# A graph network's third layer opens its dense hop with four rounds at once on the node chunks that are ready

## The chip, the cores and the metric

The kernel runs on one NeuronCore of a Trainium2 chip. The metric is the device time of one execution in microseconds (us). The core has five engines that work in parallel and hand over to each other by semaphores: TensorE (PE, matrix products and transpositions into PSUM, which has eight banks of 2 KB per partition), VectorE (DVE), ScalarE (ACT), GpSimd (POOL, which here issues the indirect DMAs) and SyncE (SP, which issues most others).

## The reference, cut to what matters

Four layers of a graph network over 3125 nodes with 64 features and 53125 edges, each `x = x + layer(relu(layernorm(x)))`. The change touches the end of the second layer, the whole third, and two small operations of the normalisation:

```python
    # second layer (L1): h @ W, weighted sums over the edges, bias, relu
    out = jax.ops.segment_sum(h[row] * norm[:, None], col, num_segments=n)
    x = x + jax.nn.relu(out + b)
    # third layer (L2): mean over the neighbours, two weight matrices
    h = jnp.maximum(_layernorm(x), 0.0)
    summed = jax.ops.segment_sum(h[src], dst, num_segments=n)
    h_neigh = summed / jnp.maximum(deg, 1.0)[:, None]
    x = x + h @ W_self.T + h_neigh @ W_neigh.T
    # fourth layer (L3): an MLP over h[src], h[dst] and edge_attr for each edge, summed by dst, an MLP per node
```

## The kernel before

**Tiling.** Nodes lie as 25 chunks of 128 (NC; chunk c holds nodes 128c to 128c+127, one per partition). At the start the kernel builds a dense adjacency matrix `A` of [128, 25 source chunks, destination nodes] in 16 bits. The first layer's three hops and the third layer's one are then "dense hops": for each of seven rounds k, 25 matmuls, one per source chunk s, sum `part(s)` (the node features split in a high and a low 16-bit half, 128 columns) times 512 destination columns of `A` into one PSUM bank. Round 6 has only 64 columns. The second layer sums over edges block by block, with windows built on the fly, into `acc_mem`; it needs room, so chunks 16 to 24 of `A` (SS = 16) are spilled to DRAM before it and reloaded after it, round by round (`reloaded{k}`, L1101), once PE has applied the last block (semaphore `applied`).

**A round.** Its steps go round the engines: PE sums 25 chunks (L1606); ACT copies the bank to SBUF (`copy_sums`, L1369); PE transposes it back to nodes (`turn_round`, L1587); DVE adds the two halves and divides by the degree (`neighbours`, L2145 and L2263); PE transposes node and neighbour features together (`turn2`, L1561); ACT copies them (`copy_turned2`, L1361); PE multiplies with the weights (`weigh2`, L1567); DVE adds the result to `xs` and normalises (`third_norm` with `centre`, L2269 and L1846 to L1851). In `dense_sums` the small PE steps of earlier rounds stand at fixed turns between a round's 25 matmuls: `turn2(k-2)` at turn 4, `turn_round(k-1)` at turn 8, `weigh2(k-2)` at turn 16. The sums of rounds alternate between two banks (seg 2 and 3), the transpositions of nodes between seg 0 and 1.

**The end of the second layer.** There are 16 blocks (NB) of four quarters. The nodes of a chunk can be finished once the last edges that lead to it are added: `EARLY_AT` lists which chunks are closed in which block (`conv1_early` on PE, `early_nodes` on DVE, eight small linked operations), the rest is closed after the last block (`conv1_late`, `late_nodes`). Chunks 0 to 5 and 10 to 17 (`READY = (6, 8)`) are closed early enough to be scaled and split before the end; they are the "ready" ones, and the hop takes them first (`L2_ORDER`). `parts_ready` counts what PE may read: first the two ready pieces, then chunks 6 to 9, then 18 to 24. Before the change only round 0 begins on the ready chunks, because each round runs through all 25 chunks in one go. `add_pairs` adds the windows of a block to `acc_mem` on DVE (L1905); the late products wait for it.

**Behind the hop.** `scale_rows(0)` and `scale_rows(1)` take the inverse roots of the two halves of the chunks (0 to 11, 12 to 24) and release the store of each half of the node table (`table_ready`, L1104 and L1118); the last layer's gathers (L1208) wait for both. Between, SP waits for `adjacency_over` and issues 14 loads of weights (L1107, L1115). All engines execute their instructions in the order in which the program writes them down; there is no scheduler.

The turns as they stand before:

```python
for turn, s in enumerate(order):
    if n == 3 and k >= 2 and turn == 4:
        turn2(k - 2)
    if 0 < k < ROUNDS - 1 and turn == 8:
        turn_round(k - 1)
    if n == 3 and k >= 2 and turn == 16:
        weigh2(k - 2)
```

## Time and profile before

| | |
|---|---|
| median of 3 runs | 1091.03 us (1090.18 to 1092.83) |
| the profiled execution | 1091.64 us |
| its span, first to last instruction | 1089.8 us |
| mean granted clock of TensorE | 0.908 |
| busy: PE, DVE, POOL, ACT | 86%, 77%, 52%, 41% |
| second layer's last block applied by PE | 552.6 to 564.4 us |
| third layer's hop | 569.2 to 618.5 us |
| second store of the node table | 631.8 us |
| first gather of the last layer | 635.8 us |

Times in rows are microseconds from the first instruction, unless marked ns. In a timeline a row gives start, duration, engine, line, operation, output and input, how many instructions were merged, and in brackets the idle time before and who ended it.
### The profile page before, as it was taken

How to read it: one execution, taken by the hardware profiler on the slowest of the kernel's cores; microseconds unless marked ns; L12 is line 12 of the kernel's file. 1: busy time of each engine (PE TensorE's matmuls, PEld its weight loads, DVE VectorE, ACT ScalarE, POOL GpSimd, SP SyncE). 2: the span in 40 equal slices, each digit the busy share in tenths (PEclk: the TensorE clock that was granted, in tenths of full speed). 3: DMA queues.
4: the chain of work that ended last, by engine and by line, in shares of the span. 5: the costliest groups of instructions: out<-in, count | busy, mean ns of one | idle time of the engine just before them, and what ended most of it. 6: DMA issues, size and time to landing. Idle time of an engine off the chain costs nothing.

```text
span 1089.8 us, 24033 instructions
## 1 busy us (share of the span) xinstructions
PE 933.4 (86%) x6195; PEld 592.5 (54%) x6195; DVE 835.1 (77%) x2627; ACT 451.3 (41%) x879; POOL 571.7 (52%) x747
## 2 busy tenths in 40 slices
PE   2788888799958878888679969999999999999995
PEld 2465655354536656676454654556555565555553
DVE  8988888743579778889974686777877877777776
ACT  2577777310105545445311234444434444434441
POOL 6534333000016777777600047777777777777770
PEclk9687777799989899989878959999999999999997
DMA  3000000600002111111125055455444544444441
GB/s 65 2 1 0 0 0 0 262 34 1 1 0 49 27 26 27 27 25 27 25 77 190 21 165 116 106 107 105 107 104 102 106 107 100 104 103 101 105 94 33
DMA packets 144600, 72.30 MB, mean 66 GB/s; under 512 B 111661, under 2 KB 136442, under 8 KB 144410
## 3 DMA queue, kind: packets, MB, share of 16 engines
q1 hardware_dynamic: 127224, 54.98, 19.3%
q0 software_dynamic: 15936, 16.35, 8.5%
q8 instruction: 30, 0.49, 0.2%
q10 hardware_dynamic: 1378, 0.22, 0.1%
q14 instruction: 32, 0.26, 0.1%
HBM read 59.13 MB, written 12.35 MB: 66 GB/s over the span
## 4 chain that ended last, share of the span: by engine, by line
PE 34%; POOL 21%; DVE 20%; issue 12%; ACT 5%; DMA 4%; DVEq 2%; ACTq 1%; POOLq 0%; SPq 0%
POOL A L1208 14%; PE seg L1606 12%; POOL pair L1208 7%; ACT A L1343 5%; PE big L1530 4%; PE seg L1733 4%; DVE A L1894 3%; PE big L1769 3%; DMA A<-table,src_i 3%; PE big L1759 2%; PE seg L1780 2%; PE seg L1801 1%; DVE acc_mem L1905 1%; PE seg L1544 1%; DVE A L1883 1%
## 5 line engine op out<-in xcount | busy, mean ns | idle before, releaser
L1208 POOL DMA_INDIRECT A<-table,src_i x338 | 323.1, 956 | 116.8 <-issue 98.6
L1208 POOL DMA_INDIRECT pair<-table,src_i x160 | 160.4, 1003 | 62.6 <-issue 48.5
L1343 ACT CAST A<-big 128x500 f32 x208 | 125.4, 603 | 48.0 <-PE big L1535 24.9
L1733 PE MATMUL seg<-A 128*128 128x384 f16 (+1 forms) x624 | 120.1, 336 | 11.1 <-DVE A L1960 8.2
L1769 PE MATMUL big<-A 128*128 128x512 f32 x208 | 109.9, 610 | 1.5 <-DMA A<-pr_table 1.5
L1636 PE MATMUL big<-A 128*128 128x300 bf16 (+1 forms) x512 | 96.5, 335 | 16.8 <-DVE A L1883 14.6
L1444 ACT COPY A<-big 128x512 f32<-128x512 f32 x104 | 60.8, 584 | 119.8 <-PE big L1759 118.6
L1450 ACT ACTIVATE A<-big,A 128x512 f32<-128x512 f32 x104 | 71.5, 688 | 93.3 <-PE big L1770 92.9
L1733 PEld LDWEIGHTS seg<-A 128*128 128x128 f16 x624 | 57.0, 98 | 89.7 <-issue 36.0
L1606 PE MATMUL seg<-A,acc_mem 128*128 128x512 f16 (+1 forms) x406 | 84.1, 362 | 7.6 <-DVEq L2124 7.6
L1271 POOL COPY cur<-pair 128x24 bf16 x100 | 39.7, 440 | 95.4 <-PE seg L1544 95.4
L1994 DVE TENSOR_TENSOR A<-seg,A 128x448 f32<-128x448 f32 x78 | 48.7, 625 | 47.6 <-PE seg L1736 31.0
L1636 PEld LDWEIGHTS big<-A 128*128 128x128 f16 x512 | 65.2, 148 | 32.9 <-DVE A L1883 15.8
L1388 ACT COPY A<-big 128x500 f32<-128x500 f32 x128 | 69.7, 569 | 29.5 <-PE big L1636 28.7
L1369 ACT ACTIVATE acc_mem<-seg 128x512 f32<-128x512 f32 (+1 forms) x28 | 15.2, 544 | 160.6 <-PE seg L1606 160.2
L1894 DVE TENSOR_SCALAR A<-iota_r,acc_mem,A 128x300 bf16<-128x300 f16 (+1 forms) x256 | 78.8, 373 | 1.6 <-PE big L1636 1.1
L1998 DVE TENSOR_REDUCE A<-A 128x64 f32<-128x448 f32 x78 | 73.6, 943 | 4.5
L1661 PE MATMUL seg<-A,cur 128*64 128x160 f32 x800 | 75.8, 325 | 0.0
L1397 ACT ACTIVATE pair<-pair,wcol 128x64 f32<-128x64 f32 x160 | 42.6, 336 | 80.3 <-DMA pair<-table,src_i 80.3
L1759 PE MATMUL big<-ident,A 128*128 128x128 f32 x416 | 64.3, 278 | 9.0 <-DMA A<-table,src_i 7.6
L2086 DVE TENSOR_SCALAR acc_mem<-iota_r,acc_mem 128x300 f16<-128x300 f16 (+1 forms) x266 | 69.4, 319 | 0.0
L1277 POOL MEMSET acc_mem<- 64x3200 f32 x1 | 2.8, 2760 | 122.9 <-PE big L1587 122.9
(306 smaller groups left out, 1780.3 us busy)
## 6 DMA issues: line engine op xcount, KB each, us to landing
A<-in_edge_attr_dram SPq DMA_DIRECT2D x103, 128.0 KB
A<-drel_flat SPq DMA_DIRECT2D x104, 126.0 KB
spilled_adjacency<-A SPq DMA_DIRECT2D x1, 7074.0 KB, 21.6
A<-spilled_adjacency SPq DMA_DIRECT2D x6, 1152.0 KB, 12.4
A<-table,src_i POOLq DMA_INDIRECT x338
A<-pr_table SPq DMA_DIRECT2D x104, 31.5 KB
pair<-table,src_i POOLq DMA_INDIRECT x160
A<-low_flat SPq DMA_DIRECT2D x78, 32.0 KB
```

The source lines that it names most:

```text
L1208: pool.indirect_dma_start(out=row, out_offset=None, in_=table, in_offset=bass.IndirectOffsetOnAxis(ap=src_i[:, tile:tile + 1], axis=0)).th ...
L1343: nc.scalar.copy(A[:, :, bass.ds(bases[k], PW)], big[:, k % 4, 0:PC].rearrange("p (s d) -> p s d", d=PW)).then_inc(window_kept, 1)
L1388: nc.scalar.copy(stage1[:, buf, :, k * PW:(k + 1) * PW], big[:, k % 4, 0:PC].rearrange("p (s d) -> p s d", d=PW)).then_inc(window_kept, 1)
L1450: nc.scalar.activation(hid_t[:, q, :], big[:, 2 + r, :], ACT.Relu, bias=mb1_sb).then_inc(hid_ready[r], 1)
L1606: op = nc.tensor.matmul(seg[:, 2 + k % 2, 0:cols], part3(s) if n == 3 else parts[:, s, :, :], A[:, s, 4 * k * P:4 * k * P + cols], start=( ...
L1636: op = nc.tensor.matmul(pair_window(k)[:, :, low:high], hot_l1[:, h, m, :, (2 * k + j) % 8], sub_hots(hot_r1, 2 * (k % 4) + j, high - low) ...
L1661: op = nc.tensor.matmul(seg[side:side + D, 2 + buf, 0:SC], cur[:, s, :], stage1[:, buf, s, :], start=(s < 2), stop=(s >= NC - 2))
L1733: op = nc.tensor.matmul(made[:, 0:held.shape[2] * D], hot_low[:, u, m, :], held[:, k, :, :], start=(m == 0 and k == 0), stop=(m == 3 and k ...
L1759: op = nc.tensor.transpose(big[:, r, j * P:(j + 1) * P], X[:, q, j, :], ident[:, :])
L1769: nc.tensor.matmul(big[:, 2 + r, :], mw1_se, x_t[:, r, :], start=True, stop=False)
L1894: op = dve.tensor_scalar(hot_r1[:, 2 * (k % 4) + j, 0:wide], iota_r[:, 0:wide], key_r[:, bass.ds(t, 1)], scale1[:, bass.ds(t, 1)], ALU.is_ ...
L1998: op = dve.tensor_reduce(X[:, q, 2, 0:D], picked.rearrange("p s f -> p f s"), AX.X, ALU.add)
```

## The change

- `EARLY_WEIGHTED` loses its last member: blocks 5 to 13 close early chunks, block 14 none. The late chunks are now 7, 8, 9 and 19, 20, 21 in one group of six and 22, 23, 24 in a group of three (before: 8, 9, 20, 21; then 22; then 23, 24).
- On PE the last block is applied in one go, and both groups of late products come after it, in banks big 2 and 3. On DVE the split of the ready chunks moves from behind the first quarter of the last step to behind the fourth, ahead of the last block's additions.
- The third hop is written out anew. Its rounds have "places": place 0 to 6 holds rounds 0, 1, 2, 3, 6, 4, 5 (`ROUND_OF`). The rounds of places 0 to 3 sum in four banks (seg 0, seg 1, big 0, big 1; `SUM_BANKS`) and begin with the 12 ready chunks that aren't spilled, all four rounds, then the two ready spilled ones (16 and 17), all four rounds. Then place by place the other eleven chunks; places 4, 5 and 6 run through all 25.
- The small steps stand at other turns (the number in brackets). Place 1: sums of place 0 transposed (4). Places 2 and 3: nodes of the place two before (1), sums of the one before (4), weighing of the one two before (7). Place 4: nodes of 2 (0). Place 5: sums of 3 (1), weighing of 2 (2), sums of 4 (3), nodes of 3 (9) and 4 (11), weighings of 3 (15) and 4 (17). Place 6: sums of 5 (4), nodes of 5 (12), weighing of 5 (18). Both node transpositions use one bank (seg 3, `TURN_BANK`), so each waits for the copy of the one before. The reloads come in the order of the places.
- `centre` has two operations fewer: the subtraction multiplies the sum by -1/64 itself, and the variance is taken once for many chunks (`variances`).
- On DVE the order of `neighbours` and `third_norm` is written out, and `scale_rows(0)` comes after `neighbours(5)`.

```diff
-EARLY_WEIGHTED = tuple(range(SIDE, SIDE + 10))
+EARLY_WEIGHTED = tuple(range(SIDE, SIDE + 9))
...
+ROUND_OF = (0, 1, 2, 3, 6, 4, 5)
+AHEAD = 4
+SUM_BANKS = (4, 5, 0, 1, 4, 5, 4)
+NODE_BANKS = (6, 2, 3, 0, 1, 2, 3)
+TURN_BANK, LATE_BANKS = 7, (2, 3)
...
+L2_UNSPILLED = tuple(s for s in L2_ORDER[0:sum(READY)] if s < SS)
+L2_SPILLED = tuple(s for s in L2_ORDER[0:sum(READY)] if s >= SS)
+L2_LATE = L2_ORDER[sum(READY):]
...
-            for k in range(ROUNDS):
+            for k in ROUND_OF:
                 cols = slice(4 * k * P, min(4 * (k + 1) * P, WIDE))
                 sp.dma_start(A[:, SS:NC, cols], spill[:, :, cols]).then_inc(ev(f"reloaded{k}"), 16)
...
+            def copy_turned2(place):
+                n = (chunks_at(place).stop - chunks_at(place).start) * P
+                act.wait_ge(ev("h_ps_L2"), place + 1)
+                if place >= 2:
+                    act.wait_ge(ev("turn2_used"), place - 1)
+                nc.scalar.copy(turn2_ring[:, place % 2, 0:n], banks[TURN_BANK][:, 0:n]).then_inc(ev("h_t_L2"), 1)
...
+            def copy_sums2(place):
+                cols = min(4 * P, WIDE - 4 * ROUND_OF[place] * P)
+                act.wait_ge(ev("sums_ps"), 3 * ROUNDS + place + 1)
+                act.wait_ge(ev("sums_nodes"), 3 * ROUNDS + place - 1)
+                nc.scalar.activation(sums_t[:, place % 2, 0:cols], banks[SUM_BANKS[place]][:, 0:cols], ACT.Copy,
+                                     scale=1.0 / SCALE).then_inc(ev("sums_t"), 1)
...
-            copy_sums(3)
-            copy_turned2(ROUNDS - 1)
+            copy_sums2(0)
+            copy_sums2(1)
+            for place in (2, 3, 4):
+                copy_turned2(place - 2)
+                copy_sums2(place)
+            copy_turned2(3)
+            copy_turned2(4)
+            copy_sums2(5)
+            copy_turned2(5)
+            copy_sums2(6)
...
+            def chunk_sums(place, s):
+
+                k = ROUND_OF[place]
+                cols = min(4 * P, WIDE - 4 * k * P)
+                if s == SS:
+                    pe.wait_ge(ev(f"reloaded{k}"), 16)
+                return nc.tensor.matmul(banks[SUM_BANKS[place]][:, 0:cols], part3(s), A[:, s, 4 * k * P:4 * k * P + cols],
+                                        start=(s == L2_ORDER[0]), stop=(s == L2_ORDER[-1]))
...
             for q in range(Q):
                 apply_block(NB - 1, (NB - 1) % 2, q, False)
-                if q == 1:
-                    pe.wait_ge(acc_step, Q + SUMS1 - PS)
-                    conv1_late(0, (8, 9, LATE_STRIDE + 8, LATE_STRIDE + 9, LATE_STRIDE + 10))
+            pe.wait_ge(acc_step, Q + SUMS1 - PS)
+            conv1_late(LATE_BANKS[0], (7, 8, 9, LATE_STRIDE + 7, LATE_STRIDE + 8, LATE_STRIDE + 9))
+
+            ready = len(PIECES) + 2 * ROUNDS
+            pe.wait_ge(ev("parts_ready"), ready + 2)
+            for s in L2_UNSPILLED:
+                chunk_sums(0, s)
             pe.wait_ge(acc_step, Q + SUMS1)
-            conv1_late(1, range(NC - 2, NC))
-
-
-            dense_sums(3)
-            for k in range(ROUNDS - 2, ROUNDS):
-                turn2(k)
-            for k in range(ROUNDS - 2, ROUNDS):
-                weigh2(k)
+            conv1_late(LATE_BANKS[1], range(NC - 3, NC))
+            for place in range(1, AHEAD):
+                for s in L2_UNSPILLED:
+                    chunk_sums(place, s)
+            for place in range(AHEAD):
+                for s in L2_SPILLED:
+                    chunk_sums(place, s)
+
+            pe.wait_ge(ev("parts_ready"), ready + 3)
+            for place in range(ROUNDS):
+                if place >= AHEAD:
+                    pe.wait_ge(ev("sums_t"), 3 * ROUNDS + SUM_BANKS.index(SUM_BANKS[place], place - AHEAD) + 1)
+                for turn, s in enumerate(L2_LATE if place < AHEAD else L2_ORDER):
+                    if place == 0 and s == SIDE + READY[1]:
+                        pe.wait_ge(ev("parts_ready"), ready + 4)
+                    if place in (2, 3) and turn == 1:
+                        turn2(place - 2)
+                    if place in (1, 2, 3) and turn == 4:
+                        turn_round2(place - 1)
+                    if place in (2, 3) and turn == 7:
+                        weigh2(place - 2)
...
+                    if place == 6 and turn == 18:
+                        weigh2(5)
+                    op = chunk_sums(place, s)
+                op.then_inc(ev("sums_ps"), 1)
+            turn_round2(6)
+            turn2(6)
+            weigh2(6)
...
-                link(dve.tensor_scalar(st_c[:, cols], st_a[:, cols], 1.0 / D, None, ALU.mult))
-                link(dve.tensor_tensor(dst_[:, cols, :], src_[:, cols, :], per_node(st_c)[:, cols, :], ALU.subtract))
+                link(dve.scalar_tensor_tensor(dst_[:, cols, :], per_node(st_a)[:, cols, :], -1.0 / D, src_[:, cols, :], ALU.mult, ALU.add))
                 link(dve.tensor_tensor(squares_, dst_[:, cols, :], dst_[:, cols, :], ALU.mult))
                 link(dve.tensor_reduce(st_c[:, cols], squares_, AX.X, ALU.add))
+
+            def variances(cols):
                 link(dve.tensor_scalar(st_a[:, cols], st_c[:, cols], 1.0 / D, EPS, ALU.mult, ALU.add))
...
+            variances(slice(0, NC))
...
                 block_step(NB, q)
-                if q == 1:
-                    for cols, parts in sides:
-                        split3(cols, parts)
-                        dve.sem_inc(ev("parts_ready"), 1)
+            for cols, parts in sides:
+                split3(cols, parts)
+                dve.sem_inc(ev("parts_ready"), 1)
+            for half in range(2):
+                add_pairs(NB - 1, (NB - 1) % 2, half, Q + SUMS1 - PS + 4 * half)
...
-            for cols in (slice(READY[0], 8), slice(SIDE + READY[1], EARLY_WEIGHTED[-1] + 1)):
-                link(dve.tensor_tensor(hs[:, cols, :], xs[:, cols, :], per_node(mean1)[:, cols, :], ALU.subtract))
+            link(dve.tensor_tensor(of_both(hs, 6, 7), of_both(xs, 6, 7), of_both(per_node(mean1), 6, 7), ALU.subtract))
             dve.wait_ge(ev("conv1_out"), 1)
-            late_nodes(big[:, 0, 0:4 * D].rearrange("p (k c d) -> p k c d", k=2, d=D), both_late,
-                       spare(4).rearrange("p (k c) d -> p k c d", k=2))
-            for half in range(2):
-                add_pairs(NB - 1, (NB - 1) % 2, half, Q + SUMS1 - PS + 4 * half)
-            late_nodes(big[:, 0, 4 * D:5 * D].rearrange("p (c d) -> p c d", d=D), lambda v: v[:, LATE_STRIDE + 10:LATE_STRIDE + 11], spare(1))
+            late_nodes(big[:, LATE_BANKS[0], 0:6 * D].rearrange("p (k c d) -> p k c d", k=2, d=D), both_late,
+                       spare(6).rearrange("p (k c) d -> p k c d", k=2))
             dve.wait_ge(ev("conv1_out"), 2)
-            late_nodes(big[:, 1, 0:2 * D].rearrange("p (c d) -> p c d", d=D), lambda v: v[:, NC - 2:NC], spare(2))
+            late_nodes(big[:, LATE_BANKS[1], 0:3 * D].rearrange("p (c d) -> p c d", d=D), lambda v: v[:, NC - 3:NC], spare(3))
...
+            def third_norm(place):
+                cols = chunks_at(place)
+                dve.wait_ge(ev("turn2_used"), place + 1)
...
                 cols = HALVES[part]
+                variances(cols)
                 invsqrt(st_b[:, cols], st_a[:, cols], st_d[:, cols])
...
-                neighbours(k)
-                if k:
-                    third_norm(k - 1)
-                if k == 3:
-                    scale_rows(0)
-                if k == 4:
-                    neighbours(5)
-                    neighbours(6)
-                    break
+            neighbours(0)
+            neighbours(1)
+            third_norm(0)
+            neighbours(2)
+            third_norm(1)
+            neighbours(3)
+            third_norm(2)
+            neighbours(4)
+            third_norm(3)
+            third_norm(4)
+            neighbours(5)
+            scale_rows(0)
+            third_norm(5)
+            neighbours(6)
             dve.sem_inc(ev("adjacency_over"), 1)
-            for k in range(4, ROUNDS):
-                third_norm(k)
+            third_norm(6)
             scale_rows(1)
             link(dve.tensor_scalar(h_parts[:, 0, :, :], hs, SCALE, None, ALU.mult))
```

PE at the end of the second layer and the start of the third's hop, before (L1661: the last block, L1649: late products, L1606: the hop, with `part3` in iota_8, acc_mem and cur):
```order
L1661 MATMUL seg<-A,cur 64x160 [waits acc_step,window_kept]
L1661 MATMUL seg<-A,cur 64x160 x12
L1649 MATMUL big<-w1_sb,acc_mem 128x64 [waits acc_step]
L1649 MATMUL big<-w1_sb,acc_mem 128x64 x4
L1661 MATMUL seg<-A,cur 64x160 x12
L1649 MATMUL big<-w1_sb,acc_mem 128x64 [waits acc_step]
L1649 MATMUL big<-w1_sb,acc_mem 128x64
L1606 MATMUL seg<-A,iota_8 128x512 [waits parts_ready,sums_t]
L1606 MATMUL seg<-A,iota_8 128x512 x5
L1606 MATMUL seg<-A,acc_mem 128x512 [waits parts_ready]
L1606 MATMUL seg<-A,acc_mem 128x512 x5
L1606 MATMUL seg<-A,acc_mem 128x512 [waits reloaded0]
L1606 MATMUL seg<-A,acc_mem 128x512
```
The same place after (L1696: the last block, L1684: late products, L1644: the hop):
```order
L1696 MATMUL seg<-A,cur 64x160 [waits acc_step,window_kept]
L1696 MATMUL seg<-A,cur 64x160 x24
L1684 MATMUL big<-w1_sb,acc_mem 128x64 [waits acc_step]
L1684 MATMUL big<-w1_sb,acc_mem 128x64 x5
L1644 MATMUL seg<-A,iota_8 128x512 [waits parts_ready]
L1644 MATMUL seg<-A,iota_8 128x512 x5
L1644 MATMUL seg<-A,acc_mem 128x512 x6
L1684 MATMUL big<-w1_sb,acc_mem 128x64 [waits acc_step]
L1684 MATMUL big<-w1_sb,acc_mem 128x64 x2
L1644 MATMUL seg<-A,iota_8 128x512 x6
L1644 MATMUL seg<-A,acc_mem 128x512 x6
L1644 MATMUL big<-A,iota_8 128x512 x6
```
The last block is no longer cut by the first late products, and behind round 0's twelve unspilled chunks stand three more rounds' twelve, in seg and big, before anything waits for a reload.

PE within a full round late in the hop, before (L1561: `turn2`, L1587: `turn_round`, L1567: `weigh2`):
```order
L1606 MATMUL seg<-A,iota_8 128x512 x3
L1561 MATMUL seg<-ident,pair 128x128 [waits h_t_L2,nb_ready]
L1561 MATMUL seg<-ident,pair 128x128 x3
L1606 MATMUL seg<-A,iota_8 128x512 x2
L1606 MATMUL seg<-A,acc_mem 128x512 x2
L1587 MATMUL big<-ident,acc_mem 128x128 [waits rows2_read,sums_t]
L1587 MATMUL big<-ident,acc_mem 128x128 x3
L1606 MATMUL seg<-A,acc_mem 128x512 x4
L1606 MATMUL seg<-A,acc_mem 128x512 [waits reloaded5]
L1606 MATMUL seg<-A,acc_mem 128x512
L1606 MATMUL seg<-A,iota_8 128x512 x2
```
After, within place 5 (L1588: `turn2`, L1602: `turn_sums`, L1594: `weigh2`):
```order
L1644 MATMUL seg<-A,iota_8 128x512
L1594 MATMUL big<-w2_t,cur 128x64 [waits h_t_L2]
L1594 MATMUL big<-w2_t,cur 128x64 x3
L1644 MATMUL seg<-A,iota_8 128x512
L1602 MATMUL big<-ident,acc_mem 64x128 [waits sums_t]
L1644 MATMUL seg<-A,iota_8 128x512 x3
L1644 MATMUL seg<-A,acc_mem 128x512 x3
L1588 MATMUL seg<-ident,pair 128x128 [waits h_t_L2,nb_ready]
L1588 MATMUL seg<-ident,pair 128x128 x3
L1644 MATMUL seg<-A,acc_mem 128x512 x2
L1588 MATMUL seg<-ident,pair 128x128 [waits h_t_L2,nb_ready]
L1644 MATMUL seg<-A,acc_mem 128x512
```
Before, a round held one of each small step; now place 5 holds two of each, and the transposition of place 4's single chunk waits for its sums two turns behind that of place 3.

DVE in one round's normalisation (st_a sum, st_c mean and then squares), before:
```order
L2269 TENSOR_TENSOR xs<-xs,big 128x256 [waits dve_chain,turn2_used]
L1846 TENSOR_REDUCE st_a<-xs 128x4 [waits rows2_read]
L1847 TENSOR_SCALAR st_c<-st_a 128x4 [waits dve_chain]
L1848 TENSOR_TENSOR pair<-xs,st_c 128x4x64 [waits dve_chain]
L1849 TENSOR_TENSOR wcol<-pair 128x256 [waits dve_chain]
L1850 TENSOR_REDUCE st_c<-wcol 128x4 [waits dve_chain]
L1851 TENSOR_SCALAR st_a<-st_c 128x4 [waits dve_chain]
```
After:
```order
L2350 TENSOR_TENSOR xs<-xs,big 128x256 [waits dve_chain,turn2_used]
L1925 TENSOR_REDUCE st_a<-xs 128x4 [waits rows2_read]
L1926 SCALAR_TENSOR_TENSOR pair<-st_a,xs 128x4x64 [waits dve_chain]
L1927 TENSOR_TENSOR wcol<-pair 128x256 [waits dve_chain]
L1928 TENSOR_REDUCE st_c<-wcol 128x4 [waits dve_chain]
```
The two operations on one column per chunk, L1847 and L1851, are gone from the round.

## Rows read from the trace of the kernel before

**Rows 1.** The page's costliest groups: line, operation | busy us, mean ns | idle before.
```profile
L1208 POOL DMA_INDIRECT A<-table,src_i x338 | 323.1, 956 | 116.8 <-issue 98.6
```

**Rows 2.** GpSimd's timeline, 545 to 665 us: start, length, line, operation, idle before.
```profile
635.78 1.01 POOL L1208 DMA_INDIRECT A<-table,src_i  x1 [13.20 <-DMA table<-pair]
```

**Rows 3.** Who waited for whom, PE, 545 to 650 us: total, times, longest.
```profile
PE big L1649 <- DVE acc_mem L1905: 7.7, 2, 3.9
```

**Rows 4.** The chain that ended last, 540 to 660 us: start, length, work.
```profile
589.81 0.44 PE big L1587 x4
...
591.97 0.84 PE big L1567 x8
592.81 2.81 PE seg L1606 x13
```

**Rows 5.** PE's timeline, 540 to 650 us.
```profile
552.61 2.10 PE L1661 MATMUL seg<-A,cur 128*64 128x160 f32 x26
...
569.16 2.77 PE L1606 MATMUL seg<-A,iota 128*128 128x512 f16 x6
...
578.82 3.00 PE L1606 MATMUL seg<-A,cur 128*128 128x512 f16 x7 [0.85 <-DVEq L2254]
...
618.54 0.78 PE L1587 MATMUL big<-ident,acc_mem 128*128 128x128 f32 x5
```

**Rows 6.** DVE's timeline, 545 to 665 us, behind the hop.
```profile
619.28 0.69 DVE L2145 TENSOR_REDUCE wcol<-big 128x256 f32<-128x512 f32 x1 [2.21 <-PE big L1587]
...
628.45 0.17 DVE L1835 TENSOR_SCALAR st_b<-st_a 128x13 int32<-128x13 int32 x1
...
630.75 1.03 DVE L2276 SCALAR_TENSOR_TENSOR pair<-pair,st_b 128x832 f32<-128x832 f32 x1
```

**Rows 7.** DVE's timeline, 545 to 665 us, ahead of the hop.
```profile
552.46 0.35 DVE L2109 TENSOR_SCALAR iota<-pair 128x384 f16<-128x384 f32 x1
...
558.48 0.28 DVE L1926 TENSOR_TENSOR pair<-seg,dinv 128x128 f32<-128x128 f32 x1
...
561.61 0.42 DVE L2227 TENSOR_TENSOR wcol<-big,dinv 128x256 f32<-128x256 f32 x1
...
562.52 0.43 DVE L2229 SCALAR_TENSOR_TENSOR xs<-wcol,xs 128x256 f32<-128x256 f32 x1
...
568.11 0.22 DVE L2227 TENSOR_TENSOR wcol<-big,dinv 128x64 f32<-128x64 f32 x1
...
570.10 0.29 DVE L2227 TENSOR_TENSOR wcol<-big,dinv 128x128 f32<-128x128 f32 x1
...
572.58 0.18 DVE L2188 TENSOR_SCALAR st_a<-st_c 128x25 f32<-128x25 f32 x1
```

**Rows 8.** SyncE's timeline, and the fourth reload with its time to landing.
```profile
564.45 17.85 SPq L1101 DMA_DIRECT2D A<-spilled_adjacency  x7
621.30 0.51 SPq L1107 DMA_DIRECT2D A<-in_L_gnn_msg_W_dram  x1
...
631.80 0.38 SPq L1118 DMA_DIRECT2D table<-pair  x1
...
L1101 SPq DMA_DIRECT2D A<-spilled_adjacency x1: 3167/3167/3167, 568.2 to 568.2; - x1
...
DMA to landing us min/median/max: 13.3/13.3/13.3
```

**Rows 9.** Windows: length, busy (count) PE, PEld, DVE, ACT, POOL, then clock, DMA, GB/s.
```profile
554.70:558.60 3.90, 0.01 (x1) 0.00 (x0) 1.66 (x11) 0.00 (x0) 0.00 (x0) 0.87 0.00 0
...
577.00:578.80 1.80, 0.96 (x4) 0.23 (x4) 1.64 (x3) 0.00 (x0) 0.00 (x0) 0.80 1.09 357
578.80:581.60 2.80, 2.78 (x7) 1.04 (x8) 0.11 (x1) 0.00 (x0) 0.00 (x0) 0.52 1.09 356
581.60:584.00 2.40, 2.40 (x14) 1.35 (x13) 0.00 (x0) 0.60 (x1) 0.00 (x0) 1.00 1.09 356
```

**Rows 10.** DVE's timeline at the first layer's end.
```profile
319.92 0.17 DVE L1851 TENSOR_SCALAR st_a<-st_c 128x4 f32<-128x4 f32 x1
```

141 lines of the change are left out of this document (76 added, 65 removed).

## The prediction

> **What bounds the kernel now.** I read the whole-run page first, then PE's waits, the windows with the granted clock, the timelines of PE and DVE around the change, and last the DMA rows. The third layer's edge loop fetches its rows with 338 indirect DMAs of GpSimd, 956 ns each, with 98.6 us of issue between them [rows 1]: some 1.25 us per gather, 423 us, from the first at 635.78 us [rows 2] to 1061 us of a span of 1089.8 us. It starts when the second half of the node table has been written, so everything ahead of that is serial, and a microsecond saved there should be one of the total. Ahead of it stands the stretch that the change rebuilds, 552 to 632 us:
> - 552.6 to 578.8 us: DVE closes the second layer in a chain of small linked operations, and PE mostly waits: 7.7 us for L1905 alone [rows 3]. PE's work there is 50 matmuls of the last block, 14 small ones, and 18 matmuls of the new hop's first round (14 from 569.16 us, 4 at 577 us).
> - 578.8 to 618.5 us: PE is full. The hop is 6 rounds of 25 matmuls of 512 columns and one of 64 columns, with three kinds of small steps between [rows 4, 5].
> - 618.5 to 631.8 us: sums, transposes and normalisation of the last rounds, one after another [rows 6].
>
> **The DVE chain before the hop.** Before, DVE does the splitting of the ready nodes (2.3 us from 552.46 us) ahead of two groups of window additions, then block 14's early nodes and two subtractions (558.48 to 561.61 us: 3.1 us), 4 late nodes (3.4 us), block 15's additions, 1 node (568.11 to 570.10 us: 2.0 us), 2 nodes (to 572.58 us: 2.5 us), and then 6.2 us of roots, scaling and splitting to PE's 578.82 us [rows 7]. After, the early nodes of block 14 and one subtraction are gone, which leaves 0.3 us of the 3.1 us: -2.8 us. The 4, 1 and 2 nodes become groups of 6 and 3. One operation of a group comes every 0.46 us for 4 nodes, 0.33 us for 2 and 0.26 us for 1, so 0.065 us more per node; for 6 and 3 nodes 0.59 and 0.39 us, seven times each and 0.2 us for the mean: 4.3 + 2.9 = 7.2 us in place of 7.8 us, -0.6 us. The splitting costs what it did, only later. Some 0.2 us of register loading is no longer covered. Sum **-3.2 us**: the last parts are ready at 575.6 us.
>
> **Is the opening hidden?** PE's own list after: the 50 block matmuls from 552.61 us at 0.081 us (26 take 2.10 us [rows 5]) end at 556.7 us; 6 late nodes, 1.3 us, 558.0 us. The split of the ready nodes ends on DVE at 558.7 us (552.5 us, 0.7 us for a register, 3.2 us for the additions, 2.3 us). Round 0's 12 unspilled matmuls at 0.2165 us (13 take 2.81 us [rows 4]) run to 561.4 us. The additions of block 15 end at 561.9 us; 3 late nodes, then 36 matmuls, 7.8 us: 570.4 us. The 8 on spilled chunks need the reloads. These start when the last block is applied, 564.45 us before, 556.75 us now. The fourth landed 568.2 + 13.3 = 581.5 us, 17.1 us after the start [rows 8], so now at 573.8 us, and the 8 are over at 574.3 us; the next four late chunks, 0.9 us, 575.2 us. That is 0.4 us ahead of the last parts (575.6 us). So 42 matmuls of rounds 1 to 3 are off the path. The cover is thin: every microsecond more of the reload or of a cold PE beyond 0.4 us counts. No other transfer runs there that could slow the reload.
>
> **The hop after the last parts.** Before, 132 matmuls of 512 columns remained: 132 x 0.2165 = 28.6 us; 7 of them took 3.00 us, 0.43 us each, at half clock [rows 5, 9], 1.5 us more; 25 of 64 columns some 0.7 us; five times a transposition of sums (0.44 us), one of nodes (as long) and a weighing (0.84 us) [rows 4], 8.5 us; a wait of 0.3 us. That is 39.7 us, and the rows give 578.82 to 618.54 us = 39.7 us. After, 90 remain: 19.5 us; 0.7 us; the small steps of places 0 to 5, of which place 4 has one chunk, 9.0 us. One stall: at place 5, turn 11 PE wants the transposition of place 4, whose sums DVE makes only after the norm of place 2 (five operations at 0.46 us behind a weighing that ends at 591.2 us); by my list DVE is done 0.8 us late. Sum 30.0 us if the clock is full. **-9.7 us**: the last hop matmul ends at 605.6 us.
>
> **The tail.** Before, 13.2 us from 618.54 to 631.78 us [rows 5, 6]. After, the last round is a full one and stands alone: copy 0.65 us, transposition 0.65 us with its drain, sum 0.70 and product 0.43 us [rows 6], transposition 0.65, copy 0.6, weighing 0.85, norm 2.3, variances 0.2, root of 11 small operations 2.3 (628.45 to 630.75 us), scaling 1.03 [rows 6], hand-overs 0.5: 10.9 us with the clock full, 12.2 us with the three PE steps at half. I take 11.5 us, **-1.7 us**, since in the tail before the clock had fallen by the second transposition. The norms of places 3 and 4 and the first half's root lie under place 6's 7.1 us of PE. SyncE then has 8.4 us of weight loads to issue after the adjacency is over (621.30 to 629.7 us, then idle to 631.80 us [rows 8]); from 608.4 us that ends at 616.9 us, 0.2 us ahead of the store at 617.1 us. Just hidden.
>
> **The mean and the variance.** A norm loses its mean and its variance operation, 0.2 us each with the gap (0.17 us [rows 10]); the subtraction becomes one that multiplies too, which the rows price alike (0.42 and 0.43 us [rows 7]). One variance over all columns returns. In the first layer's end the last two rounds run on DVE without a gap: 4 x 0.2 - 0.2 = **-0.6 us**. In the hop it is in the tail's sum.
>
> **Behind it.** PE begins the first half of the receiver rows at about 611.3 us, 5.8 us before the second half is ready, against 7.8 us before; it takes 8.1 us at half clock. DVE has 5.2 us of splitting first and takes 3.9 us for three rounds, so PE's fourth round has 1.3 us to spare. Nothing is added.
>
> **Sum.** 3.2 + 9.7 + 1.7 + 0.6 = 15.2 us off the profiled execution's 1091.64 us: 1076.4 us. The runs' median is 1091.03 us, 0.6 us below it, so 1075.8 us.
>
> **A rule weighed.** The rows on the clock: PE idle for 3.9 us before 558.6 us, and its clock was 0.50 (1.2 GHz) while it worked to 564 us; idle for most of 575 to 578.8 us, and it was 0.52 to 581.6 us, then 1.00 (2.4 GHz) [rows 9]. In the list above PE's idle stretches are 0.8, 0.6 and 2.5 us. The Trainium skill, "TensorE: Matmul & The Clock Gate", section "A second HAM failure mode: psum-queue depth-cycling", says that a kernel which cycles through PSUM banks makes PE pause often enough for its clock to swing between both levels. No row here shows four banks in a row; the two-bank rounds ran at 1.00. By that rule rival 3 would come.
>
> **Rivals.**
> 1. *Hop resumes cold.* After place 2's spilled pair PE waits for the reload and the parts, 2.5 us from 571.3 us. If the clock falls, 5 to 11 matmuls cost 0.21 us more, 1.1 to 2.4 us; with a fall in the opening too, up to 4 us. For it: the fall at 578 us came after such a stretch. Against: PE works in that stretch more than it did there. 1076.9 to 1079.8 us, say 1078 us.
> 2. *The shift is not passed on.* If PE, not DVE, sets when the receiver table is written, up to 2.3 us return (8.1 - 5.8): 1078.1 us. Against it the 1.3 us of slack.
> 3. *The opening runs at 1.2 GHz.* 36 + 8 matmuls at 0.43 us from 562.6 us end at 581.5 us, the late four at 583.2 us: 7.6 us after 575.6 us. 1083.4 us. For it: the first 14 matmuls of the hop before ran so. Against: they followed idle time.
> 4. *Slower than before.* One mechanism: the clock stays at 1.2 GHz through opening and hop. Opening 7.6 us, 90 matmuls x 0.21 = 19 us, small steps 9 us: 35.6 us more than forecast, 1111 us. It turns to a loss once the opening and 36 of the 90 run so (7.6 + 7.6 us). Only stalls at every place would cause it.
> 5. *Nothing is gained*, because the ready parts come too late for the opening. They would have to come after 573 us; they depend on DVE work that ended at 554.7 us before.
> 6. *Better.* No stall at place 5 and a full clock in the tail: 0.8 + 0.6 us, and a little from shorter waits: 1073 to 1074.5 us.
>
> **How the numbers follow.** Forecast 0.58 (1074.5 to 1077), rival 1 0.19, rival 2 0.07, rival 3 0.05, rival 4 0.02, rival 5 0.01, rival 6 0.08. The range takes the forecast with both bounds of the tail (-0.6, +0.7 us), rivals 6, 1 and 2: 1072 to 1080.5 us. A measurement here tells about 0.3%, 3.3 us, from no change; all but rivals 4 and 5 are faster than 1087.8 us: faster 0.97, same 0.01, slower 0.02.
>
> **What would show it.** Right: last parts at about 575 us (all times 0.6 us earlier by the first layer), hop matmuls of 512 columns from 558 us, clock 1.00 from 558 to 605 us, last hop matmul at 605 us, second table store at 616.5 us and the first gather of the edge loop at 620 us. Wrong: a wait for the reload beyond 576 us, a clock of 0.5 after 562 us, waits for nb_ready of over 2 us in places 5 and 6, or gathers that begin over 4 us after the store.

## The result, and the profile after

The changed kernel takes **1078.32 us** (median of 4 runs, 1077.11 to 1079.15) beside 1090.76 us of the kernel before on the same chip: ratio 0.9881 [0.9864, 0.9898], 12.4 us less. The forecast was 1075.8 us and 15.2 us less, the range 1072.0 to 1080.5 us. The direction and the place were right; the size was 2.8 us too large: the runs' interval is 11.1 to 14.8 us less, and 15.2 us lies just outside it.

The page of the kernel after, two of its lines and the row of the last layer's gathers (columns as in [rows 1]; before, the span was 1089.8 us and the row had 116.8 us of idle):

```profile
span 1077.1 us, 23987 instructions
...
PEclk9677777899988999999889969999999999999997
...
L1221 POOL DMA_INDIRECT A<-table,src_i x338 | 323.1, 956 | 114.7 <-issue 97.5
```

The edge loop's gathers cost what they did, 956 ns each. They only begin earlier. GpSimd's timeline of after, which answers to [rows 2]:

```profile
622.37 1.03 POOL L1221 DMA_INDIRECT A<-table,src_i  x1 [11.32 <-DMA table<-pair]
```

That is 13.4 us before the 635.78 us of before. PE's timeline of after, 550 to 640 us (start, length, line, operation, tile, count, idle before and what ended it), which answers to [rows 4] and [rows 5]:

```profile
553.77 3.73 PE L1696 MATMUL seg<-A,cur 128*64 128x160 f32 x50
...
559.57 1.47 PE L1644 MATMUL seg<-A,iota 128*128 128x512 f16 x6 [0.58 <-DVEq L2295]
...
572.16 0.59 PE L1644 MATMUL big<-A,acc_mem 128*128 128x512 f16 x2
574.91 0.60 PE L1644 MATMUL big<-A,acc_mem 128*128 128x512 f16 x2 [2.15 <-DMA A<-spilled_adjacency]
...
575.78 2.40 PE L1644 MATMUL seg<-A,cur 128*128 128x512 f16 x9
...
595.36 0.33 PE L1588 MATMUL seg<-ident,pair 128*128 128x128 f32 x1 [0.79 <-DVEq L2345]
...
605.25 1.67 PE L1644 MATMUL seg<-A,cur 128*128 128x512 f16 x7
...
607.71 0.63 PE L1602 MATMUL big<-ident,acc_mem 128*128 128x128 f32 x4 [0.78 <-ACT acc_mem L1389]
...
611.04 1.84 PE L1594 MATMUL big<-w_t,cur 128*128 128x64 f32 x8 [0.68 <-ACT cur L1374]
```

From 559.6 us PE works on the hop where it used to wait. Its one long pause on the opening is for the fourth reload, 2.15 us. The nine matmuls at 575.78 us hold a second, short one: the third of them starts at 576.50 us and not at 576.2 us, since DVE finishes the last parts at 576.38 us. The clock (columns as in [rows 9]):

```profile
554.00:572.00 18.00, 16.94 (x120) 10.31 (x117) 13.35 (x46) 0.00 (x0) 0.00 (x0) 1.00 0.77 250
572.00:576.00 4.00, 1.85 (x10) 0.65 (x8) 3.50 (x12) 0.00 (x0) 0.00 (x0) 1.00 1.11 301
576.00:580.00 4.00, 3.88 (x20) 1.77 (x19) 0.86 (x3) 0.60 (x1) 0.00 (x0) 1.00 1.09 360
580.00:605.00 25.00, 24.21 (x173) 16.43 (x172) 17.32 (x50) 5.70 (x11) 1.25 (x4) 1.00 0.02 5
605.00:611.00 6.00, 3.21 (x19) 1.68 (x18) 4.18 (x8) 1.18 (x2) 1.19 (x5) 1.00 0.31 68
611.00:615.00 4.00, 3.96 (x20) 3.83 (x20) 1.95 (x5) 0.96 (x2) 0.04 (x1) 0.57 0.20 49
```

It is 1.00 from the opening to the last hop matmul, and falls to 0.57 in the tail. DVE's timeline of after, which answers to [rows 6] and [rows 7]: the split of the ready nodes, the six nodes, the three, the variances, the last parts, the tail.

```profile
557.20 0.35 DVE L2189 TENSOR_SCALAR iota<-pair 128x384 f16<-128x384 f32 x1
...
562.99 0.56 DVE L2312 TENSOR_TENSOR wcol<-big,dinv 128x384 f32<-128x384 f32 x1
...
567.33 0.36 DVE L2312 TENSOR_TENSOR wcol<-big,dinv 128x192 f32<-128x192 f32 x1
...
570.26 0.18 DVE L2269 TENSOR_SCALAR st_a<-st_c 128x25 f32<-128x25 f32 x1
...
575.76 0.62 DVE L2190 SCALAR_TENSOR_TENSOR cur<-pair,cur 128x448 f16<-128x448 f32 x1
...
612.91 0.42 DVE L2350 TENSOR_TENSOR xs<-xs,big 128x256 f32<-128x256 f32 x1 [3.32 <-PE big L1594]
...
617.70 1.02 DVE L2358 SCALAR_TENSOR_TENSOR pair<-pair,st_b 128x832 f32<-128x832 f32 x1
```

SyncE's timeline of after, which answers to [rows 8]:

```profile
557.53 17.16 SPq L1114 DMA_DIRECT2D A<-spilled_adjacency  x7
...
609.78 0.51 SPq L1120 DMA_DIRECT2D A<-in_L_gnn_msg_W_dram  x1
...
618.75 0.38 SPq L1131 DMA_DIRECT2D table<-pair  x1
```

### The profile page after: what moved, and what is told of

Its sections match the earlier page's. It is cut to its first block, busy times and chain, and to the rows that moved or that the text cites. A ratio compares the mean times of both kernels' runs of the same rounds, so it can differ in the third digit from the quotient of the medians.

```text
span 1077.1 us, 23987 instructions
## 1 busy us (share of the span) xinstructions
PE 921.8 (86%) x6195; PEld 584.2 (54%) x6195; DVE 827.8 (77%) x2585; ACT 450.3 (42%) x879; POOL 574.0 (53%) x747
## 4 chain that ended last, share of the span: by engine, by line
PE 44%; DVE 21%; POOL 13%; issue 10%; ACT 5%; DMA 4%; DVEq 2%; ACTq 1%; SPq 1%; POOLq 0%
PE seg L1627 9%; POOL A L1221 7%; POOL pair L1221 6%; PE seg L1812 6%; PE big L1848 5%; PE big L1557 5%; ACT A L1356 4%; DVE A L1974 3%; PE big L1838 3%; PE seg L1859 3%; PE seg L1880 3%; PE seg L1571 2%; DMA A<-table,src_i 1%; DVE A L1963 1%; DVE acc_mem L1985 1%
## 5 line engine op out<-in xcount | busy, mean ns | idle before, releaser
L1671 PE MATMUL big<-A 128*128 128x300 bf16 (+1 forms) x512 | 93.8, 328 | 16.5 <-DVE A L1963 15.7
L1671 PEld LDWEIGHTS big<-A 128*128 128x128 f16 x512 | 64.7, 147 | 30.4 <-DVE A L1963 17.1
L1627 PE MATMUL seg<-A,acc_mem 128*128 128x512 f16 (+1 forms) x350 | 69.6, 357 | 7.7 <-DVEq L2204 7.7
L1696 PE MATMUL seg<-A,cur 128*64 128x160 f32 x800 | 72.4, 315 | 0.0
L1838 PE MATMUL big<-ident,A 128*128 128x128 f32 x416 | 64.6, 278 | 7.4 <-DMA A<-table,src_i 5.4
L1696 PEld LDWEIGHTS seg<-A,cur 128*64 128x64 f32 x800 | 53.8, 141 | 16.8 <-issue 14.3
```

The source lines that it names most:

```text
L1627: op = nc.tensor.matmul(seg[:, 2 + k % 2, 0:cols], parts[:, s, :, :], A[:, s, 4 * k * P:4 * k * P + cols], start=(s == 0), stop=(s == NC - 1))
L1671: op = nc.tensor.matmul(pair_window(k)[:, :, low:high], hot_l1[:, h, m, :, (2 * k + j) % 8], sub_hots(hot_r1, 2 * (k % 4) + j, high - low) ...
L1696: op = nc.tensor.matmul(seg[side:side + D, 2 + buf, 0:SC], cur[:, s, :], stage1[:, buf, s, :], start=(s < 2), stop=(s >= NC - 2))
L1838: op = nc.tensor.transpose(big[:, r, j * P:(j + 1) * P], X[:, q, j, :], ident[:, :])
```

## Where the 12.4 us come from, and where 2.8 us went

Both kernels were profiled three times in all (before_again, before_third, after_again and after_third are among the experiments below). The execution is cut at three marks: GpSimd's first gather of the second layer, PE's first matmul of the second layer's last block, and the issue of the second table store. All times are us, read from the timelines.

| | before | before_again | before_third | mean | after | after_again | after_third | mean | difference |
|---|---|---|---|---|---|---|---|---|---|
| start to first gather | 332.59 | 332.58 | 333.68 | 332.95 | 331.87 | 332.54 | 332.93 | 332.45 | -0.5 |
| to the last block | 220.02 | 219.35 | 219.98 | 219.78 | 221.90 | 220.60 | 219.45 | 220.65 | +0.9 |
| last block to store | 79.19 | 77.41 | 79.21 | 78.60 | 64.98 | 65.70 | 64.84 | 65.17 | -13.4 |
| store to the end | 458.00 | 457.46 | 459.03 | 458.16 | 458.35 | 459.36 | 458.88 | 458.86 | +0.7 |
| span | 1089.8 | 1086.8 | 1091.9 | 1089.5 | 1077.1 | 1078.2 | 1076.1 | 1077.1 | -12.4 |

The stretch that the change rebuilds gives 13.4 us, against 14.6 us of the forecast. Cut once more at DVE's end of the last parts and at PE's end of the last hop matmul, the means of three are (rounded, so that the differences add up to 13.5 us):

| us | before | after | difference | forecast |
|---|---|---|---|---|
| last block to the last parts | 25.8 | 22.6 | -3.2 | -3.2 |
| the hop behind the last parts | 39.7 | 31.0 | -8.7 | -9.7 |
| the tail to the second store | 13.1 | 11.5 | -1.6 | -1.7 |

The rows "to the last block" and "store to the end" run code that the change hardly touches. In all fourteen profiles of this study the second layer took 218.9 to 221.9 us and the part behind the store 455.5 to 459.4 us. The four profiles with the old hop (norms_only is the fourth) have means of 220.2 and 458.1 us there, the ten with the new hop and its variants 220.4 and 457.3 us. The +0.9 and +0.7 us of the table do not come back in this wider comparison, so they look like scatter. In the second layer the scatter is that of GpSimd's 160 gathers: their durations sum to 158.9 us in the profile with the shortest second layer (five_open, 218.9 us) and to 162.0 us in the one with the longest (after, 221.9 us).

## Experiments

All ratios are against the kernel before on the same chip. Medians of different experiments can come from different chips.

### Is the lost 2 us of the second layer chance? (after_again)

The kernel after, unchanged.

> The changed kernel once more. Between the last block's first matmul and the second table store it gained 14.2 us, yet only 12.7 us of the span, because the second layer's blocks 3 to 8 came 1.8 us later than before, with longer gathers. If that is chance, this execution has its first window additions of the blocks and the last block's first matmul closer to before (552.0 to 553 us in place of 553.8 us) and the ratio of the medians comes out at 0.986 to 0.987. If the change itself delays the blocks, the last block starts at 553.8 us again and the ratio stays at 0.988 to 0.989.

Measured: 1078.3 us (1075.55 to 1080.02), 0.9877 [0.9855, 0.9899]. The ratio lies between what chance and what a delay would have given (0.986 to 0.987 and 0.988 to 0.989), and so does the last block's start (553.14 us); by itself this run does not decide. The second layer took 220.6 us and not 221.9 us, 0.6 us more than in the profile of before, where the first profile had 1.9 us more. The fourteen profiles above answer the question. This profile shows something else, PE's timeline of after_again:

```profile
574.17 0.60 PE L1644 MATMUL big<-A,acc_mem 128*128 128x512 f16 x2 [2.05 <-DMA A<-spilled_adjacency]
...
575.05 3.94 PE L1644 MATMUL seg<-A,cur 128*128 128x512 f16 x9
```

and its windows:

```profile
572.00:576.00 4.00, 1.83 (x8) 0.63 (x8) 3.39 (x11) 0.00 (x0) 0.00 (x0) 0.92 1.12 314
576.00:580.00 4.00, 4.00 (x14) 1.54 (x14) 0.07 (x1) 0.60 (x1) 0.00 (x0) 0.65 0.95 312
```

Nine matmuls took 3.94 us here and 2.40 us in the first profile, behind the same wait and with the same short stop for the last parts: this is rival 1, the hop that resumes cold, in one execution and not in another.

### The norms alone (norms_only)

```diff
--- before
+++ norms_only
-                link(dve.tensor_scalar(st_c[:, cols], st_a[:, cols], 1.0 / D, None, ALU.mult))
-                link(dve.tensor_tensor(dst_[:, cols, :], src_[:, cols, :], per_node(st_c)[:, cols, :], ALU.subtract))
+                link(dve.scalar_tensor_tensor(dst_[:, cols, :], per_node(st_a)[:, cols, :], -1.0 / D, src_[:, cols, :], ALU.mult, ALU.add))
...
+            def variances(cols):
                 link(dve.tensor_scalar(st_a[:, cols], st_c[:, cols], 1.0 / D, EPS, ALU.mult, ALU.add))
```

> The kernel before with one part of the change: the norms have two operations fewer and the variance is taken once for many chunks. Theory: 0.6 us less at the first layer's end and 0.6 us less in the tail of the third hop (two norms there, one variance back), 1.2 us in all, 1089.6 us. Rival: the subtraction that also multiplies costs more than the plain one and nothing or less than 0.4 us is left.

Measured: 1090.13 us (11 runs, 1088.59 to 1093.26), 0.9994 [0.9979, 1.0009]: by the times the forecast 1.2 us can neither be told from nothing nor ruled out. The profiles tell more. In the first layer, from the end of the last hop matmul to the store of the table, it is 11.4 us in each of the three profiles of before, and 10.8 to 10.9 us in norms_only and in each of the ten profiles that have the new hop too: 0.5 us less, where 0.6 us were expected. The tail of the third hop is 12.1 us against 13.1 us: 1.0 us less, since three norms lie there and not two. The rival, a dearer subtraction, did not come: it takes 0.42 us in both kernels.

### The opening (open_none, open_one)

Of the change all is kept but the opening. In open_none no hop matmul starts before the last parts; in open_one only the first round opens early, as in the kernel before. So open_one is the change without the 42 early matmuls of rounds 1 to 3, and open_none lacks round 0's early matmuls as well.

```diff
--- after
+++ open_none
-            pe.wait_ge(ev("parts_ready"), ready + 2)
-            for s in L2_UNSPILLED:
-                chunk_sums(0, s)
             pe.wait_ge(acc_step, Q + SUMS1)
             conv1_late(LATE_BANKS[1], range(NC - 3, NC))
+            pe.wait_ge(ev("parts_ready"), ready + 4)
+            for s in L2_UNSPILLED:
+                chunk_sums(0, s)
```

```diff
--- after
+++ open_one
-            for place in range(1, AHEAD):
+            for place in range(1, 1):
...
-            for place in range(AHEAD):
+            for place in range(1):
                 for s in L2_SPILLED:
...
-                for turn, s in enumerate(L2_LATE if place < AHEAD else L2_ORDER):
+                for turn, s in enumerate(L2_LATE if place < 1 else L2_ORDER):
```

> The changed kernel, but PE waits for the last parts before it begins any round of the hop; order, banks and turns stay. 60 matmuls of 512 columns that ran before 576.5 us then come after it, 60 x 0.2165 = 13.0 us, and the hop starts on an idle PE at half clock, 1 to 2 us more: 1092 to 1094 us, slower than the kernel before. Rival: if the order of turns and banks brought the gain and not the opening, it stays under 1084 us.

> The changed kernel with round 0 alone begun on the ready chunks, as before the change; places 1 to 3 run through all 25 chunks when their turn comes. 42 matmuls go back behind the last parts: 9.1 us, and with 12 us of idle PE ahead of them the clock falls, 1.5 us more: 1087.4 to 1089.5 us. Rival: as for the kernel with no opening, under 1084 us.

Measured: open_none 1091.39 us (12 runs), 1.0005 [0.9994, 1.0016]; open_one 1086.3 us (6 runs), 0.9965 [0.9948, 0.9982]. PE's waits in open_none (who waited for what: total, times, longest), and its windows:

```profile
PE seg L1644 <- DVEq L2335: 12.4, 1, 12.4
```

```profile
564.00:576.00 12.00, 0.09 (x1) 0.10 (x2) 10.56 (x35) 0.00 (x0) 0.00 (x0) 0.50 1.09 342
576.00:580.00 4.00, 4.00 (x11) 1.45 (x12) 0.10 (x1) 0.00 (x0) 0.00 (x0) 0.56 0.95 309
```

Both stay above the rivals' 1084 us. In open_none DVE's chain is as short as in after, but PE waits through it, and the hop then takes 45.3 us from the end of the last parts to the end of its last matmul, where before it took 38.7 to 40.4 us. The shorter chain and tail and the longer hop nearly cancel: 80.3 us from the last block to the store, before 78.6 us in the mean. Round 0's early matmuls, which the kernel before had too, give back 5.1 us.

What the change adds is read from open_one. It is 4.8 us below before by the medians (3.8 us by the ratio), and 2.7 us in the stretch from the last block to the store (75.9 us): this is the shorter DVE chain and tail, the norms and the new turns, less a cold start of the hop. The 42 early matmuls of rounds 1 to 3 give the rest, 8.0 us of the medians from open_one to after_again, and 10.7 us of the stretch. Of that some 9.1 us is their own time. The parts of the rest (the regrouped late nodes, the order of the places, the turns) were not run one by one; the chain's -3.2 us is read from the timelines.

Both kernels landed 0.6 to 1.1 us below the low end of what was expected. In both, PE also resumes at half clock after its wait (12.4 us in open_none, 10.4 us in open_one); after shortens that wait to 2 us. PE's timeline of open_one:

```profile
572.21 1.04 PE L1644 MATMUL seg<-A,iota 128*128 128x512 f16 x2 [10.39 <-DVEq L2332]
573.03 4.23 PE L1644 MATMUL seg<-A,cur 128*128 128x512 f16 x9
```

### How thin is the cover? (reload_late)

The reloads are issued later (562.3 us, not 557.5 us), with the rest as in after.

```diff
--- after
+++ reload_late
+            sp.wait_ge(ev("conv1_out"), 2)
             for k in ROUND_OF:
```

> The changed kernel with the reload of the spilled chunks held back until the second group of late products is done, about 6.2 us later. In the changed kernel the fourth reload lands at 574.9 us and PE reaches the last parts (576.5 us) without a gap. Theory of a thin cover: the reload now lands at 581 us, PE has 0.4 us for the pair and 0.9 us for four late chunks behind it, so the last parts' matmuls begin at 582.4 us in place of 576.5 us: 5.9 us more, and a colder start of 1 to 2 us: 1084 to 1086 us. Rival, the reload has slack of its own: under 1080 us.

Measured: 1082.92 us (4 runs, 1081.52 to 1084.43), 0.992 [0.9895, 0.9946]: 4.6 us more than after, a little under the 1084 to 1086 us expected, and well over the rival's 1080 us. PE's timeline of reload_late:

```profile
571.74 0.61 PE L1645 MATMUL seg<-A,acc_mem 128*128 128x512 f16 x2 [1.31 <-DMA A<-spilled_adjacency]
...
575.06 1.03 PE L1645 MATMUL big<-A,acc_mem 128*128 128x512 f16 x2 [2.71 <-DMA A<-spilled_adjacency]
578.46 1.03 PE L1645 MATMUL big<-A,acc_mem 128*128 128x512 f16 x2 [2.37 <-DMA A<-spilled_adjacency]
...
580.14 2.91 PE L1645 MATMUL seg<-A,cur 128*128 128x512 f16 x9
```

The reloads land one after another, some 3.3 us apart, and PE waits for the last three of the four that it needs. Counted from the last block, which came earlier in this execution (552.31 us), the reloads are issued 6.3 us later than in after (10.0 us behind it, 3.8 us there), but the fourth lands only 5.1 us later: 16.1 us after the first issue, in after 17.4 us. The stretch from the last block to the store is 71.4 us, 6.5 us more than in after and after_third. Of these 5.1 us are the later landing. Another 1.3 us is the clock, which fell in these waits: two of the pairs took 1.03 us each, not 0.6 us, and the nine matmuls 2.91 us. So the later landing comes through in full, as a cover of a few tenths means, and the clock adds to it; that the sum is close to the 6.3 us of the issue is chance. The expectation had both parts, 5.9 us and 1 to 2 us. That the medians differ by 4.6 us and not by 6.5 us is within the interval of this kernel, 1080.4 to 1085.9 us by its ratio.

### The stall at place 5 (single_later)

The transposition of place 4 is asked for three turns later.

```diff
--- after
+++ single_later
-                    if place == 5 and turn == 11:
+                    if place == 5 and turn == 14:
```

> The changed kernel with one step moved: the transposition of place 4's single chunk stands at turn 14 of place 5 in place of turn 11. PE waited 0.8 us there for VectorE. Theory: the wait goes, the last hop matmul and the second table store come 0.8 us earlier, 1077.5 us. Rival: the wait moves to the next step that needs VectorE and nothing is left.

Measured: 1077.25 us (5 runs, 1074.12 to 1077.56), 0.9856 [0.9833, 0.9878]. The 0.79 us wait at 595.36 us is gone from the profile (waits for L2345 1.5 us in all, 2.2 us in after). The intervals of its ratio and of after's overlap, so by the times the 0.8 us is not told apart. Here too the hop resumed cold, so its profile is compared with after_again, which did so as well: from the last block to the store 64.9 us against 65.7 us, and the hop 31.2 us against 32.0 us. That is the 0.8 us of the theory, from one profile of each.

```profile
575.12 0.60 PE L1644 MATMUL big<-A,acc_mem 128*128 128x512 f16 x2 [2.07 <-DMA A<-spilled_adjacency]
...
575.99 3.79 PE L1644 MATMUL seg<-A,cur 128*128 128x512 f16 x9
```

### Filling the wait for the reload (five_open, five_scale, pair_later)

five_open opens a fifth round, on place 5's ready chunks, between the third and the fourth spilled pair, and so gives PE 12 matmuls (2.6 us) where it waited 2.1 us.

```diff
--- after
+++ five_open
-SUM_BANKS = (4, 5, 0, 1, 4, 5, 4)
-NODE_BANKS = (6, 2, 3, 0, 1, 2, 3)
+SUM_BANKS = (4, 5, 0, 1, 4, 6, 5)
+NODE_BANKS = (2, 3, 2, 3, 0, 1, 2)
+FIFTH = 5
...
-            for place in range(AHEAD):
+            for place in range(AHEAD - 1):
                 for s in L2_SPILLED:
                     chunk_sums(place, s)
+            for s in L2_UNSPILLED:
+                chunk_sums(FIFTH, s)
+            for s in L2_SPILLED:
+                chunk_sums(AHEAD - 1, s)
...
-                for turn, s in enumerate(L2_LATE if place < AHEAD else L2_ORDER):
+                for turn, s in enumerate(L2_LATE if place < AHEAD else L2_SPILLED + L2_LATE if place == FIFTH else L2_ORDER):
```

The turns of the small steps of places 3 to 5, the order of ACT's copies and some of PE's waits move with it. five_scale is five_open with the first half's scaling behind the sums of the last place, and the first half's table store behind the weight loads.

```diff
--- five_open
+++ five_scale
-            sp.wait_ge(table_ready, 3)
-            sp.dma_start(table_nodes[:, HALVES[0], :], hs[:, HALVES[0], :]).then_inc(table_stored, 16)
...
+            sp.wait_ge(table_ready, 3)
+            sp.dma_start(table_nodes[:, HALVES[0], :], hs[:, HALVES[0], :]).then_inc(table_stored, 16)
...
-            scale_rows(0)
...
+            scale_rows(0)
```

> The changed kernel with a fifth round (place 5's) begun on its twelve unspilled ready chunks in a fifth bank, between the other rounds' pairs and the one whose reload comes last; the node banks and the later turns are moved to make room. The twelve fill the 2.1 us in which PE waited for the reload. Theory: place 5 is 2.6 us shorter, the wait of 0.8 us there goes too, and PE does not idle, so its clock does not fall (it did in one of two profiles, 1.5 us). VectorE's chain of norms then sets the tail: 2.5 us less at the second table store, 1075.8 us, and closer to 1075 us if the falls count. Rival: VectorE sets the end of the hop already and less than 1 us is left.

> As with five rounds begun, and the first half's root and scaling moved behind the sums of the last place, into the 3.3 us in which VectorE waits for the last weighing; the store of the first half moves behind the weight loads. Theory: 0.4 to 0.8 us less than with five rounds alone, 1075.2 us. Rival: PE's first half of the receiver table starts later by what the root takes and becomes the end of the stretch: no gain or 1 us worse.

Measured: five_open 1075.41 us (6 runs, 1072.26 to 1078.46), 0.9861 [0.984, 0.9882]; five_scale 1076.27 us (5 runs), 0.9857 [0.9835, 0.9879]. PE's timeline of five_open:

```profile
569.27 1.46 PE L1645 MATMUL seg<-A,iota 128*128 128x512 f16 x6
570.57 1.46 PE L1645 MATMUL seg<-A,acc_mem 128*128 128x512 f16 x6
...
572.73 2.15 PE L1645 MATMUL seg<-A,cur 128*128 128x512 f16 x9
...
601.41 0.63 PE L1603 MATMUL big<-ident,acc_mem 128*128 128x128 f32 x4 [0.78 <-ACT acc_mem L1390]
604.34 1.11 PE L1589 MATMUL seg<-ident,pair 128*128 128x128 f32 x4 [2.30 <-DVEq L2350]
```

No gap, no cold resumption: the nine matmuls take 2.15 us. From the end of the last parts to the end of the last hop matmul it is 27.6 us, 3.0 us less than in after (30.5 us). But from the last block to the store it is 63.5 us against a mean of 65.2 us: 1.7 us remain, where 2.5 us were expected (1.4 us against the two profiles of after that did not resume cold). The tail is 13.3 us, in after 11.8 us. The new wait is 2.30 us before the last transposition, where after had 1.38 us. DVE, in five_open, is still at the norm of place 5 when PE's last sums are there:

```profile
602.63 0.42 DVE L1933 TENSOR_REDUCE st_c<-wcol 128x4 f32<-128x256 f32 x1
603.08 0.69 DVE L2230 TENSOR_REDUCE wcol<-big 128x256 f32<-128x512 f32 x1
```

With the scaling moved (five_scale) that wait falls to 1.5 us, and the stretch is 63.4 us: the forecast 0.4 to 0.8 us does not come. The root and the scaling take DVE from 606.23 to 610.45 us, and the last weighing is done at 609.85 us, so the last norm begins 0.7 us late:

```profile
609.49 0.96 DVE L2363 SCALAR_TENSOR_TENSOR pair<-pair,st_b 128x768 f32<-128x768 f32 x1
610.59 0.42 DVE L2355 TENSOR_TENSOR xs<-xs,big 128x256 f32<-128x256 f32 x1
```

Of all kernels tried, five_open has the lowest median, 1075.4 us, but single_later and five_scale on the same chip have ratios as low (0.9856 and 0.9857), and its interval overlaps that of after: an improvement on after of some 2 us is likely and not shown.

pair_later moves only place 3's spilled pair behind the late chunks of places 0 to 2:

```diff
--- after
+++ pair_later
-            for place in range(AHEAD):
+            for place in range(AHEAD - 1):
                 for s in L2_SPILLED:
...
+                if place == 3:
+                    for s in L2_SPILLED:
+                        chunk_sums(3, s)
```

> The changed kernel with the pair of spilled ready chunks of place 3 taken out of the opening and put ahead of place 3's late chunks, so that PE waits for the parts of chunks 6 to 9 and not for the fourth reload. Theory: the parts of chunks 18 to 24 bind, not the reload, so place 0 ends when it did and the pair costs its 0.43 us later: 0.4 us more, no difference that a measurement tells. Rival, the reload binds: up to 0.5 us less, and the clock falls less often.

Measured: 1078.11 us (4 runs, 1076.3 to 1079.97), 0.9884 [0.9867, 0.99], the same as after within the intervals. PE's timeline of pair_later:

```profile
575.20 0.61 PE L1644 MATMUL seg<-A,iota 128*128 128x512 f16 x2 [1.86 <-DVEq L2335]
...
577.09 1.68 PE L1644 MATMUL seg<-A,cur 128*128 128x512 f16 x7 [0.85 <-DVEq L2338]
```

The wait for the reload became two for DVE's parts, first of chunks 6 to 9, then of 18 to 24, and the clock stayed at 1.00. The hop took 31.0 us behind the last parts, 0.4 us more than in after and after_third (30.5 us), as the theory had it, since the parts and not the reload bind; by the times this is not told apart. The stretch from the last block to the store is 64.7 us.

### Both kernels again (before_again, before_third, after_third)

Both kernels unchanged, one profile each, to see how much of a difference of two profiles is the execution's own.

> The kernel before once more, for the spread of one execution's stretches. Eleven executions so far had 218.9 to 221.9 us from the second layer's first gather to its last block and 455.9 to 459.4 us behind the second table store, in code that is the same for all. If that is chance, this one lies inside both; the stretch from the last block to the second store is 77.5 to 79.2 us, by what PE's clock does between the late products.

> The kernel before a third time, as above: 77.5 to 79.2 us from the last block to the second store, 219 to 222 us ahead of it, 456 to 459 us behind it. If the changed kernel makes the second layer's blocks or the edge loop slower, its three executions lie above those of the kernel before in the same stretch.

> The changed kernel a third time: 65.0 us from the last block to the second store where the clock stays at 2.4 GHz after the wait for the reload, 65.7 us or more where it falls; 219 to 222 us ahead of it and 456 to 459 us behind it, if those stretches vary by chance.

Measured: spans 1086.8, 1091.9 and 1076.1 us; the table above has the stretches. From the last block to the store: 77.4, 79.2 and 64.8 us. The first is at the low edge of what was expected, the second at the high edge, and the third speaks for 65.0 us; its second layer took 219.5 us, which speaks against a delay in each execution. In after_third the hop did not resume cold behind a 2.06 us wait:

```profile
573.44 0.60 PE L1644 MATMUL big<-A,acc_mem 128*128 128x512 f16 x2 [2.06 <-DMA A<-spilled_adjacency]
...
574.32 0.59 PE L1644 MATMUL seg<-A,cur 128*128 128x512 f16 x2
575.14 1.68 PE L1644 MATMUL seg<-A,cur 128*128 128x512 f16 x7 [0.23 <-DVEq L2335]
```

In before_again the first matmuls after the last parts ran at full clock, where [rows 9] has 0.52. In before_third they were slow again (seven in 2.81 us, before_again 1.68 us). The windows of before_again:

```profile
576.00:580.00 4.00, 3.15 (x15) 1.28 (x14) 1.59 (x4) 0.60 (x1) 0.00 (x0) 1.00 1.09 356
```

## Why the prediction was right, point by point

- **The DVE chain, -3.2 us.** Right. From the last block's first matmul to the memset behind the last parts it was 26.3 us before (25.8 and 25.9 us in the other two profiles), and is 22.8 us in all three of after's: -3.5 us against the profile of before, -3.2 us against the mean of its three.
- **The opening is hidden.** Right. The unspilled matmuls and the first three spilled pairs were done at 572.75 us. PE then waited 2.15 us for the fourth reload, until 17.4 us after the reloads began (forecast 17.1 us). Since the last block came 1.16 us later in this execution than in the profile of before, 574.9 us is the forecast's 573.8 us. PE came to the last parts just before they were ready and stopped for 0.3 us in after and 0.4 us in after_third; the forecast had it there 0.4 us early. reload_late shows how thin that is: 5.1 us of later landing cost 5.1 us of the stretch, and the clock 1.3 us more.
- **The hop, -9.7 us.** Right in its mechanism, 1.0 us too large. From the end of the last parts to the last hop matmul's end it took 30.5 us in after and after_third (forecast 30.0 us) and 32.0 us in after_again: 31.0 us in the mean, against 39.7 us. The forecast stall at place 5, turn 11 is there at 595.36 us with 0.79 us, forecast 0.8 us. open_one shows that the 42 early matmuls are worth 8.0 us of the medians.
- **Rival 1, the cold hop.** It had 0.19 as the way the time would come out. It is a way in which some executions go: of four profiles with a wait of 2.05 to 2.15 us before the last spilled pair, two (after_again, single_later) had nine matmuls at 3.94 and 3.79 us; in the other two the clock did not fall (2.40 us in after, which holds the 0.3 us stop for the last parts). That is 1.4 to 1.5 us more, as priced (1.1 to 2.4 us), in two of four.
- **The tail, -1.7 us.** Right. It took 11.8 us in after (forecast 11.5 us), in which the clock was 0.57 and the last weighing 1.84 us; 11.7 us in after_third, and 11.1 us in after_again, where the weighing took 1.10 us: 11.5 us in the mean, against 13.1 us. norms_only has 12.1 us, so 1.0 us of it is the shorter norms.
- **The norms, -0.6 us in the first layer.** Right: -0.5 us. From the last hop matmul of the first layer to the store of its table it is 11.4 us in every profile with the old norms and 10.8 to 10.9 us in every one with the new. The times do not tell it from nothing.
- **Behind it, nothing added; rival 2.** The first gather stands 3.6 us after the second store, before 3.9 to 4.0 us. The edge loop starts earlier by all that the store does. Rival 2 did not come.
- **Rival 3, the opening at 1.2 GHz.** Did not come: 1.00 from 554 to 572 us with 16.94 us of matmuls in 18 us, through four banks in a row, and five in five_open (1.00 as well). The Trainium skill, "TensorE: Matmul & The Clock Gate", section "A second HAM failure mode: psum-queue depth-cycling", tells of a kernel that cycled through PSUM banks, with PE pausing between its groups of matmuls often enough for the clock to swing. Here PE went from bank to bank without such pauses, and no swing is seen; what the prediction made of that page, that four banks in a row would bring it, did not come.
- **Rivals 4 and 5** did not come. **Rival 6** was half there: the tail took 11.1 us in after_again, single_later and pair_later, but in after_again and pair_later with the stall, and in single_later, which has none, with a cold hop.

**The terms that were mis-sized.** The forecast took 15.2 us off one profiled execution, and 12.4 us came. Of these 2.8 us some 0.6 us lie in that execution: its 79.19 us from the last block to the store held 1.5 us for seven matmuls at half clock, which I booked as a cost that the change removes. before_third paid it too, before_again did not; the mean of three is 78.6 us. Another 0.6 us is what after needs more than forecast (65.2 us in the mean, 64.6 us forecast). It lies in the hop: 0.5 us in every profile, whose cause I did not find, and the cold resumption of after_again, another 0.5 us of the mean; the shorter chain of these profiles gives 0.3 us back. The other 1.6 us stand in the second layer and the edge loop, with code that the change leaves as it is, and they do not come back in the comparison of all fourteen profiles (+0.2 and -0.9 us). That they are scatter is argued from this, not shown. If they are, the change is worth nearer 13.9 us (13.4 us and the norms' 0.5 us), which the runs' interval holds. That the time fell so well inside the range is in part luck: such scatter, of 1 to 2 us, has no term in the prediction.

## What to carry to other kernels

When a serial stretch leaves TensorE waiting for a chain of small VectorE operations, open as many accumulations as there are free banks on the operands that are ready: here 42 matmuls moved off the path gave 8.0 us of the 12.8 us between the medians of before and after on one chip, and the same change without them (open_one) 4.8 us. Then look at what each opened group still waits for (here the fourth of seven reloads) and put one more group in front of that wait: a gap of 2 us had room for 12 matmuls, which made the hop 3.0 us shorter in five_open, and in two of four profiles the gap was followed by another 1.4 to 1.5 us at the low clock. Count first what the next chain will do with the time: of those 3.0 us only 1.4 to 1.7 us reached the store. A cost read from one profile, above all a half-clock stretch, is booked as the change's gain only if other profiles of the same kernel have it too.

## What the runs showed of the hardware

- The same wait of 2.05 to 2.15 us was followed by the low clock in two executions and by the full one in two others, with the same instructions up to it (nine matmuls 3.94 us in after_again, 3.79 us in single_later; 2.40 us in after with a stop of 0.3 us in it, and no fall in after_third, PEclk 1.00). After a wait of 10.4 us it was low in open_one (4.23 us for nine).
- PE at work on one accumulation after the other through four banks (16.94 of 18 us busy, after) and five (five_open) kept a granted clock of 1.00.
- In every one of the fourteen profiles some of the second layer's 160 gathers took 1.3 to 1.7 us instead of about 1.0 us, without a cause that the profiles show. Their sum, 158.9 to 162.0 us, goes with the length of the second layer, 218.9 to 221.9 us.
- The reloads land one by one, some 3.3 us apart, at 355 to 360 GB/s. Issued 6.3 us later (reload_late), the fourth landed 5.1 us later.
